# Seeding an accumulation bank with x/2 on ScalarE, for the output tiles 2 to 5 of a tuned FFN kernel

## The reference

```python
out = lax.conv_general_dilated(x, weight, window_strides=(1,), padding=[(4, 4)],
                               dimension_numbers=('NCH', 'OIH', 'NCH'), feature_group_count=4)
h = out + einsum('nd,od->no', c, c_weight)[:, :, None] + bias[None, :, None]   # (32, 64, 1024)
...
q = einsum('bsd,rd->bsr', h, Wq_w);  scores = einsum('bsr,er->bse', q, keys)   # 64 experts
gate = softmax over the 16 largest scores, spread back over the 64 experts, else 0
z = einsum('bsd,nd->bsn', h, A_w)            # 512 = 64 experts x rank 8
ffn = einsum('bsn,on->bso', z * gate, B_w) * 2.0
return x + ffn
```

## Time and profile before

| | us |
|---|---|
| median of 3 runs | 228.86 (227.99 to 228.99) |
| the profiled execution, its own time | 228.66 |
| its span, first to last instruction | 226.9 |
| TensorE (PE) busy | 222.9 |
| VectorE (DVE) busy | 194.5 |
| ScalarE (ACT) busy | 126.4 |

### The profile page before, as it was taken

One profiled execution on the slowest core, in us unless ns is written; L12 is line 12 of the kernel. 1 busy time (PEld: TensorE's weight loads), 2 busy tenths in 40 slices (PEclk: granted clock), 3 DMA queues, 4 the chain that ended last, 5 costly groups with the idle time before them and its releaser, 6 DMA issues.

```text
span 226.9 us, 4036 instructions
## 1 busy us (share of the span) xinstructions
PE 222.9 (98%) x1351; PEld 198.4 (87%) x1351; DVE 194.5 (86%) x443; ACT 126.4 (56%) x317; POOL 7.6 (3%) x16
## 2 busy tenths in 40 slices
PE   8999999999999999999999999999999999999995
PEld 6889998898988989889989889898998989898884
DVE  1799889999999989999999999899989995868442
ACT  4898857357274592936473856648473853252200
POOL 2010053000000000000000000000000000000000
PEclk9999999999999999999999999999999999999999
DMA  6997048659864666545261616655472337157642
GB/s 199 371 401 313 4 111 286 215 181 288 290 209 103 207 210 181 182 131 201 85 196 47 185 28 186 207 139 189 131 249 85 114 120 248 43 161 256 198 162 95
DMA packets 24869, 40.89 MB, mean 180 GB/s; under 512 B 2832, under 2 KB 11920, under 8 KB 24848
## 3 DMA queue, kind: packets, MB, share of 16 engines
q1 hardware_dynamic: 24704, 40.55, 55.4%
q10 hardware_dynamic: 144, 0.08, 0.2%
HBM read 28.04 MB, written 12.58 MB: 179 GB/s over the span
## 4 chain that ended last, share of the span: by engine, by line
PE 94%; DVE 3%; issue 1%; ACT 0%; POOL 0%; DVEq 0%; POOLq 0%
PE p_z L892 36%; PE p_conv L841 9%; PE p_out L933 6%; PE p_out L934 6%; PE p_out L941 6%; PE p_conv L785 5%; PE p_out L892 3%; PE p_out L961 3%; PE p_out L965 2%; PE p_out L963 2%; PE p_t L961 2%; PE p_conv L961 2%; PE p_t L963 2%; PE p_conv L965 2%; PE p_conv L963 2%; PE p_t L965 2%
## 5 line engine op out<-in xcount | busy, mean ns | idle before, releaser
L509 ACT ACTIVATE h_hi<-h_t 128x1024 fp32r<-128x1024 f32 x16 | 17.1, 1069 | 36.3 <-DVE h_t L1144 36.3
L892 PEld LDWEIGHTS p_z<-a_hi,h_hi 128*128 128x128 f32 x240 | 32.6, 188 | 2.1 <-DVE a_hi L1156 0.2
L892 PE MATMUL p_z<-a_hi,h_hi 128*128 128x264 f32 x240 | 34.2, 285 | 0.0
L892 PE MATMUL p_z<-a_hi,h_lo 128*128 128x264 f32 x240 | 34.1, 284 | 0.0
L892 PE MATMUL p_z<-a_lo,h_hi 128*128 128x264 f32 x240 | 33.9, 284 | 0.0
L892 PEld LDWEIGHTS p_z<-a_hi,h_lo 128*128 128x128 f32 x240 | 31.3, 188 | 0.2
L892 PEld LDWEIGHTS p_z<-a_lo,h_hi 128*128 128x128 f32 x240 | 31.0, 188 | 0.0
L1102 DVE TENSOR_TENSOR x_lo<-x_blk,x_hi 128x1536 fp32r<-128x1536 f32 (+4 forms) x18 | 25.3, 1406 | 2.3 <-ACT x_hi L509 2.2
L933 PE MATMUL p_out<-b_hi,zt_hi 128*128 128x512 f32 (+1 forms) x64 | 25.0, 393 | 0.0
L934 PE MATMUL p_out<-b_hi,zt_lo 128*128 128x512 f32 (+1 forms) x64 | 24.7, 388 | 0.0
L559 ACT ACTIVATE p_conv<-p_conv,u 128x128 f32<-128x128 f32 x88 | 23.7, 358 | 1.6 <-PE p_conv L841 1.4
(11 more groups left out here) (160 smaller groups left out, 401.1 us busy)
## 6 DMA issues: line engine op xcount, KB each, us to landing
x_nat<-in_x_rows SPq DMA_DIRECT2D x16, 512.0 KB, 4.1
out_dram<-x_nat SPq DMA_DIRECT2D x31, 256.0 KB, 3.3
x_blk<-in_x_blocks SPq DMA_DIRECT2D x14, 516.0 KB, 3.8
z_dram<-a_raw SPq DMA_DIRECT2D x64, 64.0 KB, 1.8
a_raw<-z_dram SPq DMA_DIRECT2D x16, 256.0 KB, 2.9
a_raw<-in_a_wq SPq DMA_DIRECT2D x8, 264.0 KB, 6.5
x_nat<-in_b_w SPq DMA_DIRECT2D x4, 512.0 KB, 9.1
a_raw<-in_b_w SPq DMA_DIRECT2D x2, 512.0 KB, 5.1
```

Of the source, the lines that this page charges most:

```text
L509: nc.scalar.activation(dst, src, ACT.Copy).then_inc(s, 1)
L892: mm = nc.tensor.matmul(z_bank(t, b)[:, 0:HB], h[:, t % 2, r, :], a[:, r, b * HB:(b + 1) * HB], start=k == 0 and r == 0, stop=k == 2 and r ...
```

## The change

For the tiles t = 2 to 5 (`seeded(t)`), VectorE's `add` is gone. In its place ScalarE runs two instructions for each half: `seed(t, k)` writes x/2 from `x_nat` into bank k of `p_out` before the products, which then all accumulate onto it, and `scale(t, k)` writes twice the bank back to `x_nat` after them. TensorE waits for `s_seed` where it waited for the addition of the tile before. Since ScalarE seeds a bank of tile 2 as soon as tile 1 is added, VectorE's additions of tile 1 stand earlier: both are now in round 3, one behind `split_x(6)`, the other in front of `turn_q(4)`.

```diff
+SD = 2
...
+        def seeded(t):
+            return SD <= t < FP
+
+        def part_done(t, k):
+            if seeded(t):
+                return s_scaled, 2 * (t - SD) + k + 1
+            return s_added, 2 * (t if t < SD else t - 2 * NP - (FP - SD)) + k + 1
...
             def store(t, k):
                 _, lo, hi = parts(t)[k]
-                sp.wait_ge(s_added, out_count(t, k))
+                sp.wait_ge(*part_done(t, k))
...
+            def seed(t, k):
+                dst, lo, hi = parts(t)[k]
+                act.wait_ge(*part_done(t - 1, k))
+                if k == 0:
+                    act.wait_ge(*rows_come(t))
+                nc.scalar.activation(dst, x_nat[:, t % XN, lo:hi], ACT.Copy, scale=1.0 / SCALING).then_inc(s_seed, 1)
+
+            def scale(t, k):
+                src, lo, hi = parts(t)[k]
+                act.wait_ge(s_out, out_count(t, k))
+                nc.scalar.activation(x_nat[:, t % XN, lo:hi], src, ACT.Copy, scale=SCALING).then_inc(s_scaled, 1)
...
@@ ScalarE's round i, behind split_z and the later weight splits @@
+                if SD + 2 <= i <= FP + 1:
+                    scale(i - 2, 0)
+                elif i == FP + 2:
+                    scale(FP - 1, 1)
                 if TB < i < TB + 3:
                     split_bt(i - TB - 1)
                 if TB + 2 <= i < TB + 4:
                     split_bt(i - TB)
+                if SD + 1 <= i <= FP:
+                    seed(i - 1, 0)
...
                 if i + 2 < NT:
                     split_h(i + 2)
+                if SD + 2 <= i <= FP:
+                    scale(i - 2, 1)
+                if SD + 1 <= i <= FP:
+                    seed(i - 1, 1)
...
@@ TensorE @@
+                elif seeded(t):
+                    pe.wait_ge(s_seed, 2 * (t - SD) + k + 1)
                 elif k < 2 and t >= 1:
-                    pe.wait_ge(s_added, out_count(t - 1, k))
+                    pe.wait_ge(*part_done(t - 1, k))
...
-                    nc.tensor.matmul(dst, zt_hi[:, block, c % 2, :], b_hi[:, c, cols], start=c == 0, stop=False)
+                    nc.tensor.matmul(dst, zt_hi[:, block, c % 2, :], b_hi[:, c, cols], start=c == 0 and not seeded(t), stop=False,
+                                     skip_group_check=seeded(t))
...
@@ VectorE's round i @@
-                if i <= FP + 1:
+                if i <= SD + 1:
                     add(i - 3, 1)
...
                     split_x(i + 3)
+                if i == SD + 1:
+                    add(i - 2, 0)
...
+                if i == SD + 1:
+                    add(i - 2, 1)
                 if TS <= i + 1 < NT - 1:
                     turn_q(i + 1)
-                if i <= FP + 1:
+                if i <= SD:
                     add(i - 2, 0)
-                elif i == FP + 2:
-                    add(FP - 1, 1)
-                elif i % 2 == 0:
+                elif FP + 4 <= i and i % 2 == 0:
                     add_22(m)
-                elif i < NT - 1:
+                elif FP + 3 <= i < NT - 1:
                     add_11(m)
```

More of the change, by code:

```diff
@@ L238, in adaln_ffn @@
         s_added = sem("s_added")
+        s_seed = sem("s_seed")
+        s_scaled = sem("s_scaled")
         block = ctx.enter_context(nc.Block())
@@ L622, in copy_xy @@
                 if m == 0:
-                    act.wait_ge(s_added, out_count(FP - 1, 1))
+                    act.wait_ge(*part_done(FP - 1, 1))
                 elif m < NP - 1:
@@ L932, in out_high @@
                     block = zt_first(t) + c // 2
-                    nc.tensor.matmul(dst, zt_hi[:, block, c % 2, :], b_hi[:, c, cols], start=c == 0, stop=False)
-                    nc.tensor.matmul(dst, zt_lo[:, block, c % 2, :], b_hi[:, c, cols], start=False, stop=False)
+                    nc.tensor.matmul(dst, zt_hi[:, block, c % 2, :], b_hi[:, c, cols], start=c == 0 and not seeded(t), stop=False,
+                                     skip_group_check=seeded(t))
+                    nc.tensor.matmul(dst, zt_lo[:, block, c % 2, :], b_hi[:, c, cols], start=False, stop=False,
+                                     skip_group_check=seeded(t))
             def out_low(t, k):
@@ L940, in out_low @@
                         pe.wait_ge(*b_lo_done(c))
-                    mm = nc.tensor.matmul(dst, zt_hi[:, zt_first(t) + c // 2, c % 2, :], b_lo[:, c, start:stop], start=False, stop=c == JC - 1)
+                    mm = nc.tensor.matmul(dst, zt_hi[:, zt_first(t) + c // 2, c % 2, :], b_lo[:, c, start:stop], start=False, stop=c == JC - 1,
+                                          skip_group_check=seeded(t))
                 mm.then_inc(s_out, 1)
@@ L971, in product_1 @@
                 if m == 0:
-                    pe.wait_ge(s_added, out_count(FP - 1, 0))
+                    pe.wait_ge(*part_done(FP - 1, 0))
                 elif m < NP - 1:
```

## The result

The changed kernel takes 229.08 us (median of 12 runs, 228.69 to 229.39) against 228.34 for the kernel before in the same session (12 runs, 227.69 to 228.99): ratio 1.0031, 95% interval 1.0020 to 1.0043. That is slower, by less than the 0.5% that I had set as what can be told from no change. The forecast of 229.2 us was meant against 228.86; as a difference it was +0.40 us, and the measured ratio makes +0.71 us (0.46 to 0.98) of it. That the two absolute figures lie within 0.12 us is in part luck: 228.86 was the median of the first three runs alone, 0.52 above that of all twelve, and the difference came out 0.31 larger than forecast. The profiled execution took 229.23 us with a span of 227.4, 0.5 longer than before.

What follows compares the result with a forecast made beforehand. TensorE was taken as the bound, with only its waits for the query to win. The terms +1.01 + 0.19 - 0.25 - 0.41 - 0.14 give +0.40 us on 228.86: 229.2 us, with 8 in 10 from 228.1 to 230.2.

Steps and rivals of the forecast that it cites:

- What bounds the kernel: Whole kernel: TensorE, busy 222.9 of 226.9 us, is the bound; freeing VectorE pays only where TensorE waits for it.
- the three waits for `q_t`: TensorE before the output matmuls of tiles 6, 8 and 9: 0.25, 0.41 and 0.30 us lost, together 0.96.
- The price of seed and scale: ScalarE: 0.6 us for each seed or scale, 0.52 to the next start; 16 make 8.3 us, hidden.
- Round 3, the loss: Before tile 4: addition, seed and `take_q(4)` in a row make `q_t` 1.80 us late; TensorE loses 1.01.
- the spare: How late `q_t` may come without delaying TensorE: 0.79 us at tile 4, 0.05 at tile 5.
- The lower bound: Round 3: without `seed(2, 1)` in the way, `q_t` is 0.56 us late, below the spare 0.79, so the loss is 0.
- Rounds 4 to 9, the return: Tiles 5 to 9: with each round 0.55 us shorter on VectorE, TensorE changes by +0.19, -0.25, 0, -0.41, -0.14 us.
- The finer rules: VectorE, rounds 4 to 9: a removed addition gives back 0.36 us behind `take_first`, 0.19 between `q_x` and `q_c`, not 0.56.
- ScalarE's queue as the bound: Rival, chance 0.13: in rounds 4 to 6 scale and seed before `take_q(i+1)` delay the query; +2.2 us, 231.0.
- Relief without the handover: Rival, chance 0.17: tile 4's late query is hidden and only the three waits go, 0.96 us won: 227.9.
- The whole: Sum over tiles 4 to 9: +0.40 us, with nothing costed outside the rounds; forecast chance 0.55.

Runs made afterwards that it cites:

- e4: The kernel before with VectorE's additions of tiles 2 to 5 only 8 columns wide, no extra work on ScalarE: 227.54 us, ratio 0.9960.
- e1: The changed kernel with `seed(2, 1)` moved behind `spread_q(4)` on ScalarE: 227.89 us, ratio 0.9979 to the kernel before.
- e3: The kernel before with only VectorE's two additions of tile 1 moved as in the change, no seeds: 229.03 us, ratio 1.0021.
- e2: e1 with VectorE's second addition of tile 1 also moved, behind `turn_q(4)`: 227.81 us, ratio 0.9964 to the kernel before.
- e6: The changed kernel with SD = 3, so tiles 3 to 5 are seeded and the handover falls before tile 5: 229.79 us, ratio 1.0063 to the kernel before.
- e5: The kernel before with 16 extra 128x512 copies on ScalarE at the places of the seeds and scales, into an unread block: 228.87 us, ratio 1.0022.
- e9: The kernel before with e5's 16 extra ScalarE copies made 8 columns wide: 229.10 us, ratio 1.0035.
- e10: e5 again, unchanged, in a later session: 228.94 us, ratio 1.0019 to the kernel before.
- e7: The changed kernel again, unchanged, in another session: 229.07 us, ratio 1.0031 to the kernel before.

## Why the prediction was right

*What bounds the kernel.* Right: TensorE's 222.9 us didn't move, and the three waits for `q_t` are all that can be won. e4 takes VectorE's load away and gains 0.9 us, for 0.96 added up from the earlier trace rows.

*The price of seed and scale.* 0.58 to 0.60 us for a seed and 0.57 to 0.58 for a scale, as the nearest rows had it. By the figures that the Trainium skill gives ("VectorE: DVE Perf Modes", section on the errata) I had put 0.61 and 0.57 beside them; the traces agree to 0.03 (that table is for writes to SBUF, and a seed writes to a bank). To the next start it was 0.47 to 0.54 us where nothing had to be waited for, but 0.61 from each `scale(i-2, 1)` to the `seed(i-1, 1)` behind it. The seed overwrites the bank that the scale reads, and waits for its end (`part_done(t - 1, k)`). In round 4:

```profile
76.00 0.58 ACT L636 ACTIVATE x_nat<-p_out 128x512 f32<-128x512 f32 x1
76.61 0.60 ACT L631 ACTIVATE p_out<-x_nat 128x512 f32<-128x512 f32 x1
```

`q_s` followed at 77.15, so the pair held ScalarE for 1.15 us where the prediction had 2 x 0.52 = 1.04. It cost nothing here.

*Round 3, the loss.* Worked out 1.01 us, seen 1.07 (0.03 of the difference is the addition, which took 0.68 us for 0.65), and the chain is the one written down: addition, seed, `q_s`, `q_x`, `q_hi`, `q_c`, `q_t`, each start within 0.25 us of the clock time forecast, of which 0.15 is the later start of the execution. e1 shows the seed's place to be the cause by undoing it (+0.20 in place of +1.07), e3 shows what VectorE's two additions cost without it (+0.20 at this tile), e2 undoes both (0.00). e6 shows the other half of the argument, the spare: the same handover before a tile with 0.05 us to spare costs 1.81, where tile 4 with 0.79 lost 1.07. The lower bound that the prediction gave this term was wrong: 0 if the seed did not stand in the way. It took off 0.56 for the addition that no longer stands between `q_x` and `q_c`, where by its own next paragraph that one gives back 0.19. With 0.19, `q_t` is 0.93 late and TensorE loses 0.14; e1 and e3 lost 0.20. Most of what the order costs is one instruction in front of `take_q(4)`: from e1 to the change it is 0.87 us at tile 4 and 0.89 at tile 9.

*Rounds 4 to 9, the return.* Worked out +0.19, -0.25, 0, -0.41, -0.14; seen +0.20, -0.24, -0.01, -0.41, -0.19. The finer rules (0.36 given back for an addition that sits in a dependency's gap, 0.19 for the one in the round trip) carried this, and they show in the idle times: VectorE's `q_c` now waits 0.30 us for `q_hi`, which the addition used to fill.

*The rivals.* ScalarE's queue as the bound didn't come. In the changed kernel `q_s` ended 0.63 us before VectorE came to turn it in round 4 (some 0.5 forecast), 0.67 in round 5 and 0.10 in round 6, where it had waited for TensorE's matmuls and not for a seed. In e5 it is 0.59 us early in round 4, and no tile is late. Relief without the handover is e2 and e4, another order of the same instructions.

*The whole.* The stretch gives +0.42, the forecast +0.40. The measured +0.71 (0.46 to 0.98) does not quite reach down to either; some 0.3 us on the middle value are not in the sum. I had costed nothing outside the rounds. It isn't the time around the span, which is that of the kernel before (1.83 and 1.82 us), and the tail is no longer than before (98.51 us for 98.58). So it would have to arise in the first 22 us, as by the same reasoning the larger part of the extra of e5, e9 and e10 does. The order of the instructions accounts for some 0.4 of the 0.7 us. The cause of the rest is open; the ratio stood at 1.0031 in two sessions (e7: 0.43 to 0.98 us), so it is not likely to be chance alone.

## What to carry to other kernels

When work moves to an engine with time to spare, its total there says little (16 instructions, 8 us, made no tile late in e5, though that kernel took 0.5 us longer for a reason not found); what the traces show to matter is where the one instruction stands that must wait for the engine it was taken from. If the head of a tight path stands behind it in the same queue, the path inherits that wait: put the handover behind the path, and let the path go first. Before moving an instruction out of a gap (behind a dependency, in a round trip to another engine), count what it really occupies: here 0.36 and 0.19 us of 0.56, so its removal gives less than its duration, and putting it into the open costs all of it.

## What the runs showed that I had not expected

Sixteen more instructions on ScalarE that disturb no tile made the kernel 0.4 to 0.8 us longer (ratios 1.0022, 1.0019 and 1.0035 in e5, e10 and e9), the same for copies of 8 columns as for 512, and outside the stretch in which they run. On the mean of the runs 0.17 us of it is time around the span (1.99 to 2.01 us for 1.82 to 1.83); the rest must, since the profiles are steady from there on, come in the first 22 us, before any of these instructions has run. The cause is open.
